# A two-layer cross-attention kernel: the first layer's softmax rows are normalised after the mix instead of before it

## The reference, cut to what matters

```python
def _L0_xattn_ref(query, key, value, Wq, bq, Wk, bk, Wv, bv, Wo, bo, mask):
    q = (query @ Wq.T + bq).reshape(Bt, St, 16, 8).transpose(0, 2, 1, 3)
    k = (key @ Wk.T + bk).reshape(Bt, -1, 16, 8).transpose(0, 2, 1, 3)
    v = (value @ Wv.T + bv).reshape(Bt, -1, 16, 8).transpose(0, 2, 1, 3)
    scores = jnp.einsum('bhqd,bhkd->bhqk', q, k) / math.sqrt(8)
    scores = jnp.where(mask, scores, neg_inf)
    attention = jax.nn.softmax(scores, axis=-1)
    out = jnp.einsum('bhqk,bhkd->bhqd', attention, v)
    return out.transpose(0, 2, 1, 3).reshape(Bt, St, 128) @ Wo.T + bo
...
x = x + tanh(g_xattn[0]) * _L0_xattn_ref(_layernorm(x), ctx, ctx, ...)
x = x + tanh(g_ffn[0]) * _L0_ffn_ref(_layernorm(x), weight)      # Hadamard, 4-bit rows, ternary weight
x = x + tanh(g_xattn[1]) * _L1_xattn_ref(_layernorm(x), ctx, ctx, ...)   # 16 heads of depth 64
x = x + tanh(g_ffn[1]) * _L1_ffn_ref(_layernorm(x), ...)         # 32 experts, top 4, and a shared one
```

## Time and profile before

| | |
|---|---|
| median of 3 runs | 270.9 us (269.98 to 271.8) |
| the profiled execution | 270.38 us, its span in the trace 268.4 us |
| PE busy | 251.5 us, 94% |
| PEld busy | 199.2 us, 74% |
| DVE busy | 211.8 us, 79% |
| ACT busy | 189.2 us, 70% |
| POOL busy | 181.6 us, 68% |
| granted TensorE clock | 0.999 |

### The profile page before, as it was taken

The page is one execution under the profiler, slowest core; times in us unless marked ns, Lnnn a source line. Parts: engine busy times, 40 slices in busy tenths (PEclk is TensorE's granted clock), DMA queues, the critical chain, the costliest instruction groups (busy, mean ns, idle before and its releaser), DMA issues. The chain is left out here.

```text
span 268.4 us, 6705 instructions
## 1 busy us (share of the span) xinstructions
PE 251.5 (94%) x1903; PEld 199.2 (74%) x1903; DVE 211.8 (79%) x656; ACT 189.2 (70%) x452; POOL 181.6 (68%) x271
## 2 busy tenths in 40 slices
PE   7888999999789999989999999999979999989994
PEld 5655667776657777768777788777767768979993
DVE  3899899999999896799667877777798624995773
ACT  2488889998799777857776767678776754555652
POOL 7367999985879766746743585448847695964480
PEclk9999999999999999999999999999999999999999
DMA  6557473400025854644584766756542051212530
GB/s 190 203 187 266 170 239 117 120 0 4 1 52 126 177 116 98 144 89 109 132 215 114 188 171 167 196 146 177 126 116 61 5 159 39 76 45 69 180 92 20
DMA packets 25987, 32.91 MB, mean 123 GB/s; under 512 B 4000, under 2 KB 18144, under 8 KB 25824
## 3 DMA queue, kind: packets, MB, share of 16 engines
q1 hardware_dynamic: 25520, 32.27, 44.3%
q10 hardware_dynamic: 432, 0.22, 0.4%
HBM read 14.32 MB, written 3.47 MB: 66 GB/s over the span
## 5 line engine op out<-in xcount | busy, mean ns | idle before, releaser
L631 POOL TENSOR_SCALAR probs<-probs,rsum 128x512 f32<-128x512 f32 x128 | 88.3, 697 | 53.3 <-DVE rsum L987 52.5
L774 ACT ACTIVATE probs<-masked,neg_max 128x512 f32<-128x512 f32 x128 | 91.8, 718 | 12.9 <-DVE neg_max L978 10.0
L1302 PE MATMUL bank<-ident,probs 128*128 128x128 f32 x512 | 78.5, 276 | 2.3 <-DVE probsT L995 1.0
L1302 PEld LDWEIGHTS bank<-ident,probs 128*128 128x128 f32 x512 | 58.6, 141 | 18.7 <-issue 10.3
L978 DVE CUSTOM_DVE_ANT_0 masked<-bank,mask 128x512 f32<-128x512 f32 x64 | 43.8, 685 | 15.3 <-PE bank L1438 14.7
L783 ACT ACTIVATE probsT<-bank 128x512 f32<-128x512 f32 x74 | 43.6, 589 | 16.0 <-PE bank L1302 15.6
L1475 PE MATMUL bank<-probsT,val 128*32 128x256 f32 (+1 forms) x512 | 46.6, 384 | 0.0
L978 DVE CUSTOM_DVE_ANT_0 masked<-bank,shared 128x512 f32<-128x512 f32 x64 | 43.4, 679 | 0.4 <-PE bank L1431 0.3
L995 DVE COPY probsT<-bank 128x512 f32<-128x512 f32 x54 | 36.8, 681 | 8.8 <-PE bank L1302 8.5
L1475 PEld LDWEIGHTS bank<-probsT,val 128*32 128x32 f32 (+1 forms) x512 | 24.4, 123 | 17.7 <-issue 4.4
L1431 PE MATMUL bank<-parts 128*128 128x512 f32 x64 | 31.2, 487 | 2.7 <-DVE neg_max L978 1.4
(11 more groups left out here) (255 smaller groups left out, 521.6 us busy)
## 6 DMA issues: line engine op xcount, KB each, us to landing
k_both<-k_low SPq DMA_DIRECT2D x32, 128.0 KB, 2.8
k_both<-k_high SPq DMA_DIRECT2D x32, 128.0 KB, 2.8
q<-q_split SPq DMA_DIRECT2D x32, 128.0 KB, 2.4
probsT<-staged_gate SPq DMA_DIRECT2D x32, 128.0 KB, 2.9
q<-q_split SPq DMA_DIRECT2D x32, 64.0 KB, 2.1
parts<-staged_k SPq DMA_DIRECT2D x7, 256.0 KB, 2.6
w_flat<-in_w SPq DMA_DIRECT2D x1, 1536.0 KB, 7.5
staged_k<-k_high SPq DMA_DIRECT2D x2, 512.0 KB, 3.1
```

What stands on the lines that cost most here:

```text
L631: pool.tensor_scalar(p, p, rsum[:, u % NCOL:u % NCOL + 1], 1.0, ALU.mult, ALU.mult).then_inc(normed, 1)
L774: act.activation(probs[:, u % NP, :], masked[:, u % NS, :], ACT.Exp, scale=-1.0, bias=neg_max[:, c:c + 1], accum_out=sums[:, c:c + 1]).the ...
L1302: ins = pe.transpose(dst[0:rows, t * P:t * P + P], src, ident[:, :])
```

## The change

In layer 0, POOL's `norm` and DVE's `recip` are left out, and `turn(u)` waits for `exp(u)` itself. The exponentials' sums are kept in `sums0` (128x64, a column per unit). When a batch's 32 units are through, DVE at step `k.end` (32 and 64) makes `recip_batch`: for each of the two query tiles one reciprocal of 128x128 elements, the 16 head sums each read 8 times over, into `tmp`. A new job `turn_sums` at step `k.end + 1` (33 and 65) transposes the two tiles on PE and copies them on ACT to `xqT` (128x256). DVE's `scaled_mix` at step `copy_at` takes the place of ACT's `mix_copy` for blocks 3 and 7: mix bank times `xqT` into `mixT`. Values get their bias when the values job is emptied (an add on DVE with the row `bv_row` in `tmp`, which a new DMA brings at the start, instead of a copy). `on_act` for layer 0 is now "odd and not 3 modulo 16": the copies of units 3, 19, 35 and 51, and of 36, 46 and 48, go from ACT to DVE, which makes 36 of layer 0's 64 copies then, after 29 before. The two new jobs also shift the numbers of the jobs behind them by one and by two, and with them the banks of the jobs of steps 60 to 65.

```diff
+        plan.setdefault(k.end + 1, []).append(("turn_sums", k.b))
         plan.setdefault(k.out_at, []).append(("out", k.b))
...
 def on_act(u):
+    if u < L1_AT:
+        return u % 2 == 1 and u % 16 != 3
     return u % 2 == 1 or u in MORE_ON_ACT
...
+            sp.dma_start(bv_row, a["bv_row"].partition_broadcast(P)).then_inc(ld["bv0"], 16)
             sp.dma_start(had[:, :], a["hadamard"]).then_inc(ld["had"], 16)
...
             for t in range(-LEAD, TOTAL):
-                if 0 <= t + LEAD - 3 < TOTAL:
+                if 0 <= t + LEAD - 3 < L1_AT:
+                    pool.wait_ge(exped, t + LEAD - 2)
+                if L1_AT <= t + LEAD - 3 < TOTAL:
                     norm(t + LEAD - 3)
...
+                if u < L1_AT:
+                    act.activation(probs[:, u % NP, :], masked[:, u % NS, :], ACT.Exp, scale=-1.0,
+                                   bias=neg_max[:, c:c + 1], accum_out=sums0[:, u:u + 1]).then_inc(exped, 1)
...
+                elif name == "turn_sums":
+                    act.activation(xqT[:, :], job_bank[:, 0:SQ], ACT.Copy).then_inc(free, 1)
...
-                    if t == k.copy_at and (k.layer or k.g == 3):
+                    if t == k.copy_at and k.layer:
                         mix_copy(k)
...
+            def recip_batch(k):
+                rows = sums0[:, k.end - L1_AT // B:k.end].rearrange("p (g h t) -> p t h g", g=4, t=NQ)
+                dve.wait_ge(exped, k.end)
+                for t in range(NQ):
+                    dve.reciprocal(tmp[:, t, :].rearrange("p (h g c) -> p h g c", h=4, g=4),
+                                   rows[:, t, :, :].unsqueeze(3).to_broadcast([P, 4, 4, 8])).then_inc(sums_ready, 1)
+
+            def scaled_mix(k):
+                n = mixes(k)
+                dve.wait_ge(mixed, k.m + 1)
+                dve.wait_ge(*freed(("turn_sums", k.b)))
+                dve.tensor_tensor(mixT[:, n % 2, :], mix_bank[:, 0:SQ], xqT[:, :], ALU.mult).then_inc(mix_copied, 1)
...
-                    dve.tensor_copy(v_flat, job_bank[:, :].rearrange("p (k c) -> p k c", k=NK)).then_inc(free, 1)
+                    dve.wait_ge(ld["bv0"], 16)
+                    dve.tensor_tensor(v_flat, job_bank[:, :].rearrange("p (k c) -> p k c", k=NK),
+                                      bv_row.unsqueeze(1).to_broadcast([P, NK, P]), ALU.add).then_inc(free, 1)
...
-                if 0 <= t + LEAD - 3 < TOTAL:
+                if L1_AT <= t + LEAD - 3 < TOTAL:
                     recip(t + LEAD - 3)
+                for k in (BLOCKS[3], BLOCKS[7]):
+                    if t == k.end:
+                        recip_batch(k)
+                    if t == k.copy_at:
+                        scaled_mix(k)
...
+                elif name == "turn_sums":
+                    pe.wait_ge(sums_ready, NQ * (j[1] + 1))
+                    ins = turn_tiles(job_bank, [tmp[:, t, :] for t in range(NQ)])
...
             def turn(u):
-                pe.wait_ge(normed, u + 1)
+                if u < L1_AT:
+                    pe.wait_ge(exped, u + 1)
+                else:
+                    pe.wait_ge(normed, u + 1 - L1_AT)
```

More of the change, by code:

```diff
@@ L54 @@
 for _name, _n in (("bq0", 1), ("bk0", 1), ("bq00", 1), ("bk00", 1), ("bq1", 8), ("bk1", 8), ("gates", 4), ("lo_k", 1), ("lo_q", 1),
-                  ("neg_half", 4), ("bv0", 1), ("bv1", 8)):
+                  ("neg_half", 4), ("bv1", 8)):
     COL[_name], NCOLS = slice(NCOLS, NCOLS + _n), NCOLS + _n
@@ L265, in build @@
         bq00, bk00 = cols[:, COL["bq00"]], cols[:, COL["bk00"]]
-        bq0, bk0, bv0, bq1, bk1, bv1 = (cols[:, COL[n]] for n in ("bq0", "bk0", "bv0", "bq1", "bk1", "bv1"))
+        bq0, bk0, bq1, bk1, bv1 = (cols[:, COL[n]] for n in ("bq0", "bk0", "bq1", "bk1", "bv1"))
         neg_half = cols[:, COL["neg_half"]]
@@ L288, in build @@
         rsum = sb("rsum", [P, NCOL])
+        sums0 = sb("sums0", [P, L1_AT])
         probsT = sb("probsT", [P, 2, 4, NK, SQ])
@@ L371, in build @@
         yT = tmp[:, :, :].rearrange("p t c -> p (t c)")
+        bv_row = tmp[:, 0, :]
         low_flat = k1_low[:, :, :].rearrange("p i k -> p (i k)")
@@ L392, in build @@
         ld = {n: sem("ld_" + n) for n in (
-            "x0", "x1", "ctx0", "ctx1", "cols", "ident", "had", "w00", "w0", "w0v", "bo0", "m0", "w1", "bo1", "m1", "fw", "wg", "moe0", "moe1", "moe2")}
+            "x0", "x1", "ctx0", "ctx1", "cols", "ident", "had", "w00", "w0", "w0v", "bo0", "bv0", "m0", "w1", "bo1", "m1", "fw", "wg", "moe0", "moe1", "moe2")}
         late_ready = sem("late_ready")
@@ L409, in build @@
         recipped = sem("recipped")
+        sums_ready = sem("sums_ready")
         normed = sem("normed")
@@ L628, in norm @@
             def norm(u):
-                pool.wait_ge(recipped, u + 1)
                 p = probs[:, u % NP, :]
+                pool.wait_ge(recipped, u + 1 - L1_AT)
                 pool.tensor_scalar(p, p, rsum[:, u % NCOL:u % NCOL + 1], 1.0, ALU.mult, ALU.mult).then_inc(normed, 1)
@@ L746, in _ @@
                 if t == TOTAL // 2 + 8:
-                    pool.wait_ge(normed, t + LEAD - 2)
+                    pool.wait_ge(normed, t + LEAD - 2 - L1_AT)
                     publish_late(pool.memset(ones32[:, :], 1.0))
@@ L770, in exp @@
                     act.wait_ge(turned, u - NP + 1)
-                if u >= NCOL:
-                    act.wait_ge(recipped, u - NCOL + 1)
+                if u >= L1_AT + NCOL:
+                    act.wait_ge(recipped, u - NCOL + 1 - L1_AT)
                 c = u % NCOL
-                act.activation(probs[:, u % NP, :], masked[:, u % NS, :], ACT.Exp, scale=-1.0,
-                               bias=neg_max[:, c:c + 1], accum_out=sums[:, c:c + 1]).then_inc(exped, 1)
+                if u < L1_AT:
+                    act.activation(probs[:, u % NP, :], masked[:, u % NS, :], ACT.Exp, scale=-1.0,
+                                   bias=neg_max[:, c:c + 1], accum_out=sums0[:, u:u + 1]).then_inc(exped, 1)
+                else:
+                    act.activation(probs[:, u % NP, :], masked[:, u % NS, :], ACT.Exp, scale=-1.0,
+                                   bias=neg_max[:, c:c + 1], accum_out=sums[:, c:c + 1]).then_inc(exped, 1)
             def copy_turned(u):
@@ L793, in mix_copy @@
                     act.wait_ge(projected_out, n - 4)
-                bias = bv1[:, k.g:k.g + 1] if k.layer else bv0[:, 0:1]
-                act.activation(mixT[:, n % 2, :], mix_bank[:, 0:SQ], ACT.Identity, bias=bias).then_inc(mix_copied, 1)
+                act.activation(mixT[:, n % 2, :], mix_bank[:, 0:SQ], ACT.Identity, bias=bv1[:, k.g:k.g + 1]).then_inc(mix_copied, 1)
             def job(j):
@@ L984, in recip @@
                 dve.wait_ge(exped, u + 1)
-                if u >= NCOL:
-                    dve.wait_ge(normed, u - NCOL + 1)
+                if u >= L1_AT + NCOL:
+                    dve.wait_ge(normed, u - NCOL + 1 - L1_AT)
                 dve.reciprocal(rsum[:, c:c + 1], sums[:, c:c + 1]).then_inc(recipped, 1)
+            def recip_batch(k):
[9 more added lines that the diff above has]
+                dve.tensor_tensor(mixT[:, n % 2, :], mix_bank[:, 0:SQ], xqT[:, :], ALU.mult).then_inc(mix_copied, 1)
             def copy_turned(u):
@@ L1633, in lay_out @@
         cols[:, COL[n]] = f[w].reshape(8, P).T
-    cols[:, COL["bv0"]] = f["L0_xattn_bv"].reshape(4, 4, 8).transpose(1, 0, 2).reshape(P, 1)
+    new["bv_row"] = f["L0_xattn_bv"].reshape(4, 4, 8).transpose(1, 0, 2).reshape(P)
     cols[:, COL["bv1"]] = f["L1_xattn_b_V"].reshape(8, P).T
```

## The result

The changed kernel took 276.9 us (median of 4 runs, 276.23 to 277.59) against 271.0 us (269.98 to 271.8): a ratio of 1.022, 95% interval 1.019 to 1.025. It is slower by 6 us, where I had forecast 2 (272.9) and a range that ended at 275.4. The profiled execution took 276.56 us, its span is 274.5 us, 6.1 more than before.

What follows compares the result with a forecast made beforehand. DVE's instruction stream was taken to set the pace in layer 0, PE in layer 1. The terms -1.7+2.4+0.34-0.3+1.25 summed to +2.0 us, forecasting 272.9 us against the median of 270.9, range 270.0 to 275.4.

Steps and rivals of the forecast that it cites:

- (a): Layer 0, steps -3 to 32: 36 small reciprocals go, two copies come, one small operation shortens; counted as -1.7 us.
- (c): Steps 33 to 52: 20 reciprocals go, four copies come, a DVE wait for ACT goes; together +0.34 us.
- (d): Steps 53 to 60: eight reciprocals go, -0.60 us, half realised as PE is filling up: -0.3 us.
- (b): Batch 0's reciprocals at step 32: two of 0.94 us delay PE's `turn(33)` and the mix: +2.4 us.
- `k_high`'s wait: Steps 33 to 52: DVE's wait of 0.5 us for ACT's `k_high` goes, -0.50 us.
- lost savings: Rival, chance 0.22: DVE's small savings end in holes at the mixes, copies and batches cost in full: +4.0, 274.9 us.
- (e): Batch 1 at step 64, PE-bound: PE stands until the values copy ends, then makes two transposes: +1.25 us.
- late absorption: Rival, chance 0.06: batch 1's cost is given back in waits that layer 1 has anyway: 271.6 us.
- (f): Values' add, new DMA, POOL's other work, and shifted banks in steps 60 to 65: no cost of their own.
- Cheap batches: Rival, chance 0.17: the 128x128 reciprocals cost what other 128-wide operations do: -0.3, 270.6 us.
- both cheap and freed: Rival, chance 0.05: all PE's waits for POOL were on the path and the batches are cheap: -2.5, 268.4 us.

Runs made afterwards that it cites:

- only what is removed: Kernel before without layer 0's POOL norms and small DVE reciprocals, values' bias added at the values, no normalisation in their place: 268.8 us, ratio 0.993.
- with the new copies: Kernel before with layer 0's normalisation left out, plus the change's sharing of copies (36 on DVE instead of 29): 271.7 us, ratio 1.004.
- PE kept busy: Changed kernel with five matmuls, their output overwritten, ahead of `turn_sums`' wait in batch 0: 275.2 us, ratio 1.016.
- the old copies: Changed kernel with layer 0's turned copies shared as in the kernel before (29 on DVE instead of 36): 273.0 us, ratio 1.009.

## Why the prediction was wrong

Two steps of it failed: the worth of the removed work in (a), (c) and (d), -4.67 us forecast and -1.96 measured, and the clock behind the stop in (b), which had no term and cost 1.74 us. The ledgers of the runs give each term a measured value.

| term | forecast | measured | from |
|---|---|---|---|
| removal (reciprocals, norms, `veps`) | -4.67 | -1.96 | only what is removed |
| seven copies, less `k_high`'s wait | +3.01 | +3.28 | with the new copies, less that |
| batch 0's stop | +2.4 | +2.28 | mix 2 to 3, PE kept busy, less with the new copies |
| the clock behind it | none | +1.74 | mixes 2 to 4, changed kernel less PE kept busy |
| batch 1 | +1.25 | +1.02 | mix 6 to 7, changed kernel less with the new copies |
| rest | none | -0.31 | left over |
| sum | +1.99 | +6.05 | |

(The forecast column sorts (a), (c) and (d) anew: -1.7 less the 1.17 of two copies is -2.87, and -1.50 and -0.3 make -4.67; copies are 1.17+2.34-0.50.)

**Wrong: the worth of the savings in (a), (c) and (d).** I priced 64 slots and `veps` at 5.22 us, took some 0.5 us off for holes, and got 2.7 us too much. Two things failed, about equally. First, DVE's work fell by 3.79 us and not 5.22: a small reciprocal holds DVE for 0.06 us, not 0.075 (the whole round of 1.94 against 1.82 us tells it better than the single distances of 0.68 and 0.605 that I had taken), and POOL's split took 0.63 us back (below). Second, the rule that nearly every saved slot is followed at once by more of DVE's work: 1.83 us went into longer waits, where I had allowed 0.55. Waits of 2.2 us in 74 seemed few, but DVE waits at the mix, at a block's end, and where it does, PE has set the pace of the block before it: what DVE saves in that block can land in the wait. The distance from mix 1 to mix 2, where DVE had 7.07 us of 8.22 and PE 7.94, shows it. I had read the windows of one block, where DVE happened to be at 7.85. My rival "lost savings" named this mechanism, and I gave it 0.22. Its sum was wrong by its own words: with (a) at nothing it also dropped (a)'s copies, 1.17 us, though it says that copies cost in full. With them it is +5.2 and 276.1, beyond the end of my range. It holds in part only: the removal did earn 1.30 us up to mix 2, within (a), and from mix 3 to mix 5, where (c) counts 1.50, it earned 0.34.

**Missing: the clock in (b).** The stop itself was right in place and size: PE released by `tmp` after 2.41 us, `turn(33)` later by 2.3 when both are counted from mix 2, reciprocals of 0.9 us each for the 0.94 I took. What I left out, a term of 1.74 us, is what a stop can do to the instructions behind it. In the trace, the granted clock was 1.00 until PE had stood from 53.2 to 55.6 us, and 0.54 and then 0.50 from 56 us on; mix 3 ran at 1.2 GHz. Filling the stop with idle work kept it at 1.00 and gave back 1.75 us of time. The Trainium skill, "TensorE: Matmul & The Clock Gate", section "Part 1: The HAM clock gate (the "warmup" mystery)", says that TensorE's clock has two states, half rate when it has been idle and full rate when busy, and that the moment of the switch varies from run to run. The trace agrees on the two states, 0.50 and 1.00 of 2.4 GHz. By that page the stop had to be priced with what follows it. That the fall is not fixed by the program alone is what the six executions with the old copies show, with mean clocks of 0.990 to 0.997; in the profiled one it came 16 us behind the stop of 2.42 us.

**Right: the copies.** 3.01 forecast, 3.28 measured. It is the largest single cost. By the distances, the copy of unit 3 cost 0.73 us, that of 19 cost 0.36, 35 and 36 together 0.89, 46 and 48 together 1.25 (0.33 of it POOL's split), and that of 51 nothing, as forecast. The 0.50 for `k_high`'s wait was not measured by itself.

**Right: (e).** 1.25 forecast, 1.02 measured; and the releaser was the values copy, one of the two that I named. Layer 1 gave nothing back, so late absorption falls.

**Half right: (f) and `veps`.** The values' add, the new transfer and the banks cost nothing that the trace shows, and `veps` is at 0.17 us in all three of its places between 8 and 112 us. But "POOL's other work comes no later than before" was half of the question. Without the norms it comes earlier. The split of step 42, and the scaling of a bias behind it, moved onto the quantisation of the residual, where two small operations of DVE took 0.96 us more beside them (0.96 and 0.33 against 0.16 and 0.17). In the table this lies inside the removal and the copies. Moving the split gave 1.01 us back. The mechanism is the one that the earlier trace rows show and that I used in the change's favour only.

**Cheap batches** and **both cheap and freed** fall with the 0.9 us of each reciprocal.

Two things stay open. What decides that the clock falls after one stop of 2.4 us and not after another of the same length was not settled; the runs show both. And the removal's -1.96 was not split by experiment into norms and reciprocals.

## What to carry to other kernels

Where an engine waits once per block for another, read the windows from landmark to landmark, one for each block, before pricing a saving: the wait's length is not the measure of what will be lost in it. And take a small instruction's slot from two streams that differ in it alone: 0.158 us, 0.075 and 0.06 were three prices of one reciprocal. A stop of TensorE costs its length and may cost half the clock behind it, so a step that serves PE is best issued where the queue ahead of PE is still full, and kept short: here batch 0's division cost 4.0 us as it was, 1.6 issued early, 1.5 made narrow and 0.4 with both (mix 2 to mix 4, less the removal with the same sharing of the copies). After taking work from an engine, look for what that engine now does sooner, and beside whom.

## What the hardware showed that I had not expected

- The clock fell to 0.50 for some 3.4 us after one stop of 2.41 us (by the windows; in the kernel with the old copies also for 3.4 us, from 71 us on), and a mix of 32 matmuls took 3.08 us instead of 1.93. PE's busy time shows 1.00 in those windows; only the clock column gives it away.
- DVE's reciprocal: 0.158 us for 128x1, 0.35 for 128x32, 0.55 for 128x64 (from PSUM), some 0.9 for 128x128. A line at 6 ns per element holds over all four. Spreading 32 columns to 2x128 by copies took 0.42 us for two, so inverting before spreading saved 0.95 us of 1.68.
- An operation of DVE on 128x2 elements in SBUF took 0.96 to 1.01 us when it met POOL's 1.01 us `TENSOR_TENSOR`, and 0.16 without it, while masks and copies with PSUM as their source stayed at 0.67 to 0.69 us, with POOL busy or idle.
